# Moving the attention outputs and score maxima off TensorE's transposes and onto DMA, and dealing the freed places out again

## The reference

```
x = layernorm(x + self_attention(x))          # iterated three times, 16 heads of 16
x = layernorm(x + cross_attention(x, ctx))    # 1601 context rows a batch, 16 heads of 16
x = layernorm(x + ffn(x))                     # 8 encoders, the best by its loss picks one adapter

# cross attention, for each of 8 batches and 16 heads:
scores = (q @ k.T) / sqrt(16)                 # 512 x 1601
attn   = softmax(scores)                      # needs the maximum and the sum of each of 512 rows
out    = attn @ v                             # 512 x 16
x2     = (out of all heads, 512 x 256) @ Wo.T
```

## Time and profile before

| what | value |
|---|---|
| median of 3 runs | 1702.16 us |
| the profiled execution | 1697.87 us |
| its span, first to last instruction | 1696.1 us |
| mean granted TensorE clock | 0.991 |
| TensorE busy | 1619.5 us, 95% |
| VectorE busy | 1235.1 us, 73% |
| ScalarE busy | 1062.5 us, 63% |
| DMA engines, mean | 116.58 MB moved, 69 GB/s |

### The profile page before, as it was taken

The page is one execution under the profiler, slowest core; times in us unless marked ns, Lnnn a source line. Parts: engine busy times, 40 slices in busy tenths (PEclk is TensorE's granted clock), DMA queues, the critical chain, the costliest instruction groups (busy, mean ns, idle before and its releaser), DMA issues.

```text
span 1696.1 us, 25766 instructions
## 1 busy us (share of the span) xinstructions
PE 1619.5 (95%) x9848; PEld 607.4 (36%) x9848; DVE 1235.1 (73%) x1790; ACT 1062.5 (63%) x2012; POOL 161.5 (10%) x151
## 2 busy tenths in 40 slices
PE   6779999999999999999999999999999999999987
PEld 5442323432333334333334334333334333332234
DVE  6787777877778777877778767877778777776423
ACT  2227676766666666676666766676666766666651
POOL 7311000100010000100010000100001000000000
PEclk9889999999999999999999999999999999999999
DMA  5673170706135160715317070623407050420000
GB/s 154 118 161 71 34 137 5 127 25 121 43 68 91 54 105 12 128 37 104 60 42 109 21 134 24 102 63 81 82 9 131 25 86 26 83 31 2 4 25 16
DMA packets 101342, 116.58 MB, mean 69 GB/s; under 512 B 21834, under 2 KB 86987, under 8 KB 101220
## 3 DMA queue, kind: packets, MB, share of 16 engines
q1 hardware_dynamic: 98484, 113.89, 34.1%
q10 hardware_dynamic: 2736, 1.06, 0.3%
HBM read 80.12 MB, written 34.78 MB: 68 GB/s over the span
## 4 chain that ended last, share of the span: by engine, by line
PE 83%; DVE 6%; ACT 5%; issue 5%; DMA 1%; POOL 1%; ACTq 0%; SPq 0%; POOLq 0%; DVEq 0%
PE banks L1107 22%; PE values L1126 22%; PE banks L1081 11%; PE work L990 5%; PE work L1004 5%; ACT xprobs L1263 4%; PE work L947 4%; PE work L1011 3%; PE work L1017 3%; PE work L932 3%; DVE xneg_max_pieces L1451 2%; PE work L1020 1%; PE work L996 1%; PE work L1029 1%; DVE xv_rows L1409 1%
## 5 line engine op out<-in xcount | busy, mean ns | idle before, releaser
L1263 ACT ACTIVATE xprobs<-banks 128x512 f32<-128x512 f32 x1664 | 902.4, 595 | 440.5 <-PE banks L1107 425.6
L1451 DVE TENSOR_REDUCE xneg_max_pieces<-banks 128x2 f32<-128x1024 f32 x768 | 910.0, 1220 | 273.2 <-PE banks L1081 271.1
L1107 PE MATMUL banks<-xq_stacks,xk_stacks 99*128 99x512 bf16 (+1 forms) x1664 | 523.3, 385 | 16.2 <-ACT xprobs L1263 8.5
L1126 PE MATMUL values<-xprobs,xv_rows 128*17 128x512 f32 x3328 | 437.9, 598 | 1.0 <-ACT xprobs L1263 1.0
L1107 PEld LDWEIGHTS banks<-xq_stacks,xk_stacks 99*128 99x128 bf16 (+1 forms) x1664 | 128.9, 97 | 412.3 <-ACT xprobs L1263 281.3
L1081 PE MATMUL banks<-xk_stacks,xq_stacks 49*128 49x512 bf16 (+1 forms) x2048 | 249.7, 335 | 10.7 <-DVE xneg_max_pieces L1451 9.0
L1081 PEld LDWEIGHTS banks<-xk_stacks,xq_stacks 49*128 49x128 bf16 x2048 | 56.8, 94 | 273.7 <-DVE xneg_max_pieces L1451 156.0
L1518 POOL TENSOR_TENSOR xk_parts<-xk_rest,xk_parts 128x401 bf16<-128x401 f32 (+1 forms) x64 | 59.0, 921 | 705.4 <-ACT xk_parts L1224 705.4
L1126 PEld LDWEIGHTS values<-xprobs,xv_rows 128*17 128x17 f32 x3328 | 55.1, 95 | 120.4 <-issue 118.9
L1513 POOL TENSOR_TENSOR xrstd<-xrstd,mhalf 128x4 f32<-128x4 f32 x23 | 23.2, 1010 | 647.5 <-DVE xrstd L1323 647.5
L1004 PE MATMUL work<-xvT,ctxT_a 128*128 128x128 f32 (+1 forms) x416 | 57.2, 282 | 3.1 <-DVE xk_rest L1384 2.0
(11 more groups left out here) (301 smaller groups left out, 1062.6 us busy)
## 6 DMA issues: line engine op xcount, KB each, us to landing
xk_stacks<-key_parts_dram SPq DMA_DIRECT2D x186, 200.1 KB, 11.8
key_parts_dram<-xk_parts SPq DMA_DIRECT2D x144, 100.0 KB, 1.7
xq_stacks<-parts_dram SPq DMA_DIRECT2D x186, 64.0 KB, 8.1
ctxT_a<-in_ctxT SPq DMA_DIRECT2D x4, 1601.0 KB, 7.2
ctxT_b<-in_ctxT SPq DMA_DIRECT2D x4, 1601.0 KB, 7.5
parts_dram<-xq_parts SPq DMA_DIRECT2D x45, 128.0 KB, 2.0
key_parts_dram<-xk_parts SPq DMA_DIRECT2D x48, 100.2 KB, 4.8
xa<-in_x SPq DMA_DIRECT2D x8, 512.0 KB, 14.2
```

The costliest lines, as they stand in the source:

```text
L1107: pe.matmul(scores[n % SRING], kst[0:ROWS[par], k, h2, par, t * P:(t + 1) * P], qst[0:ROWS[par], k, h2, par, :], start=True, stop=True).th ...
L1126: last = pe.matmul(av[32 * j:32 * j + HD + 1, :], vals[:, k, t, gr * GH + j, :], probs[:, sl % 2, j, :], start=t == 0, stop=t == XKT - 1)
L1263: nc.scalar.activation(probs[:, sl % 2, j, :], scores[n % SRING], ACT.Exp).then_inc(exped, 1)
L1451: nc.vector.tensor_reduce(nmp[:, of % 2, j2, :, q, piece], pairs[n % MRING][:, :, :], AX.X, ALU.max, negate=True).then_inc(on["mxr"], 1)
```

## The change: what it does

- The jobs `otr`, `oT` and `max` are gone. IN_BETWEEN keeps one job (`v` 3, now in slot 19).
- `x1T`, `x2T` (two each) and `loss` are moved from IN_BETWEEN to slot ends of their own. To make the room, `xo` 0, `xo` 1, `qproj` 0 and `mid` go from 2 parts to 1, and `gram` 2 from 3 to 2. SLOT_END is put in a new order.
- The outputs of a group go from `oS` by four DMAs of 16 rows into `oT` (dims by tokens), with the sums spread by a fifth over 128 partitions. VectorE inverts 16 columns (`invert`), SyncE sends the inverses to DRAM and reads them back, each row 16 times, and VectorE multiplies (`scale`, 64 partitions x 512). `xo` reads `oT`.
- The maxima are turned by VectorE (a transpose in blocks of 32 x 32, one more step of `dve_max_parts`), and SyncE, not ScalarE, sends them to DRAM and into the stack (`sp_max_rows`).
- In the last group all four scores stand ahead of the products and go through a ring of 6 banks.
- At the end of the program only the last group's outputs are still turned on TensorE; the half of `xo` that doesn't need them is done before.

```
-        IN_BETWEEN = {
-            1: ("otr", 3, PREV), 2: ("oT", 0, PREV), 4: ("oT", 1, PREV), 8: ("x1T", 0, NEXT), 10: ("max", 1, NOW),
-            11: ("x1T", 1, NEXT), 12: ("x2T", 0, PREV), 14: ("otr", 0, NOW), 16: ("x2T", 1, PREV), 18: ("v", 3, NOW),
-            23: ("max", 2, NOW), 27: ("otr", 1, NOW), 35: ("loss", 0, PREV), 36: ("max", 3, NOW),
-            41: ("otr", 2, NOW), 49: ("max", 0, NEXT),
-        }
+        IN_BETWEEN = {19: ("v", 3, NOW)}
         SLOT_END = [
+            (("kproj", 0, NEXT), 1), (("kproj", 1, NEXT), 1), (("v", 0, NOW), 2), (("v", 1, NOW), 2),
+            (("xo", 0, PREV), 1), (("xo", 1, PREV), 1), (("x1T", 0, NEXT), 1), (("x1T", 1, NEXT), 1),
...
         VECTOR_WORK = {
+            1: [("invert", "o", 3, PREV)], 4: [("aggr", "x1", 0, NEXT)],
+            14: [("invert", "o", 0, NOW)], 18: [("scale", "o", 0, NOW)],
+            27: [("invert", "o", 1, NOW)], 32: [("scale", "o", 1, NOW)],
+            40: [("invert", "o", 2, NOW)], 44: [("scale", "o", 2, NOW)],
+            5: [*norm_steps("apply", "x1", 0, 2, NEXT), ("scale", "o", 3, PREV)],
...
+            elif name == "invert":
+                m = GROUPS * b + q
+                v.wait_ge(moved, N_MOVED * (m + 1))
+                v.reciprocal(rs[:, m % 2, :], rs[:, m % 2, :]).then_inc(inverted, 1)
+            elif name == "scale":
+                v.wait_ge(spread, 16 * (m + 1))
+                v.tensor_tensor(oT[these, k, :], oT[these, k, :], rsb[these, :], ALU.mult).then_inc(scaled, 1)
...
+        def sp_max_rows(of):
+            sp.wait_ge(on["comb_ready"], n)
+            sp.dma_start(g.max_dram.rearrange("r (b c) -> b r c", c=32), mrow[:]).then_inc(on["mrow_out"], 16)
+            sp.wait_ge(on["mrow_out"], 16 * n)
+            for par in range(2):
+                sp.dma_start(qst[row:row + 2, k, gr * GH // 2:(gr + 1) * GH // 2, par, :], src[par])
...
+        def sp_move_outputs(m):
+            sp.wait_ge(evac, m + 1)
+            sp.dma_start(rs[:, m % 2, :], oS[HD::2 * HD, :].rearrange("j (s x) -> j s x", x=GH * T // P)).then_inc(moved, 16)
+            for j in range(GH):
+                row = half * P // 2 + j * HD
+                sp.dma_start(oT[row:row + HD, k, :], oS[2 * HD * j:2 * HD * j + HD, :]).then_inc(moved, 16)
+
+        def sp_spread_inverses(m):
+            sp.wait_ge(inverted, m + 1)
+            sp.dma_start(g.rsum_dram[m % 2].rearrange("j (s x) -> (j s) x", x=GH * T // P), rs[:, m % 2, :]).then_inc(rs_out, 16)
+            sp.wait_ge(rs_out, 16 * (m + 1))
+            sp.dma_start(rsb[these, :], g.rsum_dram[m % 2].unsqueeze(1).broadcast_to([GH, HD, T])).then_inc(spread, 16)
...
+        def score_bank(n):
+            if n < LAST_SCORE:
+                return scores[n % SRING], SRING
+            place = n - LAST_SCORE
+            return g.banks[:, place % LAST_RING, :], before
...
             elif name == "xo":
                 if part == 0:
-                    pe.wait_ge(on["w_free"], ph.order.after(("oT", 1, b)))
-                last = rows_of(W, x2T, xoT, i, units(part, parts, 2 * CH))
+                    pe.wait_ge(scaled, GROUPS * (b + 1))
+                last = rows_of(W, oT, xoT, i, units(part, parts, 2 * CH))
```

More of the change, by code:

```diff
@@ L1158, in act_job @@
             name, i, b = job
-            on_scalar = ("oT", "x1T", "x2T", "kproj", "qproj", "enc", "mid", "wdT", "gw", "x1T head", "qproj rest",
+            on_scalar = ("x1T", "x2T", "kproj", "qproj", "enc", "mid", "wdT", "gw", "x1T head", "qproj rest",
                          "qproj head")
@@ L1369, in dve_job @@
             name, i, b = job
-            on_vector = ("kproj", "qproj", "xo", "y", "gram", "loss", "max", "otr", "qproj rest", "qproj head")
+            on_vector = ("kproj", "qproj", "xo", "y", "gram", "loss", "qproj rest", "qproj head")
             if name not in on_vector and not (name == "v" and not ph.first):
@@ L1491, in dve_slot @@
             if parts:
[L1492 to L1493 removed]
+                for step in range(1, 4):
+                    dve_max_parts(MAIN, m + 1, step)
             if todo:
@@ L1617, in sp_stacks @@
                 sp_query_stacks(c, top)
+                if top and between is not None:
+                    sp_spread_inverses(between)
                 sp_key_stacks(b, c, top)
@@ L2001, in dve_front @@
                 if n == MXG:
-                    for step in range(3):
+                    for step in range(4):
                         dve_max_parts(FIRST, 0, step)
-                    dve_job(FIRST, ("max", 0, 0))
                 elif n - 1 in BETWEEN_TILES and n < MXG:
@@ L2041, in cross_attention_and_ffn @@
         tail_w = (g.W[:], g.banks[:, 4, :])
+        tail_oT = (g.banks[:, 4, :], g.banks[:, 5, :])
+        tail_xo = [g.banks[:, q, 0:D] for q in range(QT)]
+        ox = rsb.rearrange("p (q n) -> p q n", q=QT)
         tail_enc = [g.banks[:, i, :] for i in range(NPAIR)]
@@ L2050, in pe_tail, with xo @@
             pe.wait_ge(loop["w_free"], len(MAIN.order.names))
+            def xo(c, first, last):
+                for q in range(first, last):
+                    one = pe.matmul(tail_xo[q], oT[:, c, q * P:(q + 1) * P], xoT[:, c, :], start=c == 0, stop=c == CH - 1)
+                return one
+            pe.wait_ge(scaled, B * GROUPS - 1)
+            xo(0, 0, 2)
             pe.wait_ge(evac, B * GROUPS)
             transposes(g.W[:], oS[:].rearrange("p (q n) -> p q n", q=QT), 0).then_inc(t_otr_made, 1)
+            xo(0, 2, QT)
             pe.wait_ge(t_ox_in, 1)
-            for c in range(CH):
-                transposes(tail_w[c], ox, c).then_inc(t_oT_made, 1)
-            for one in t_oT_in:
+            for q in range(QT):
+                one = pe.transpose(tail_oT[q // 2][:, q % 2 * P:(q % 2 + 1) * P], ox[:, q, :], ident[:])
+                if q % 2:
+                    one.then_inc(t_oT_made, 1)
+            for i, one in enumerate(t_oT_in):
                 pe.wait_ge(one, 1)
-            for i in range(2):
-                rows_of(tail_w[i], x2T, xoT, i, range(2 * CH)).then_inc(t_xo_made, 1)
+                xo(1, 2 * i, 2 * i + 2).then_inc(t_xo_made, 1)
             pe_keep_busy(pe, KEEP_NORM, g.banks[:, 5, :])
```

207 lines of the change are left out of this document (111 added, 96 removed).

## The result

| kernel | median | lowest to highest | against before, 95% interval |
|---|---|---|---|
| before | 1701.23 us | 1699.74 to 1702.57 | |
| changed | 1655.38 us | 1651.15 to 1656.91 | 0.9727, 0.9706 to 0.9748 |

A forecast was written before the change was run, and what follows sets the result against it. TensorE bounds the kernel, slot by slot. Full batches -27, batch 0 -5, batch 7 -4.4, last group -5.4, end -2.0, start -1.3 sum to -45 us: 1655 us forecast, own range 1647 to 1664, 8-in-10 range 1641 to 1674.

The forecast's parts named there:

- The slot rule: Loop slots: 0.99 + what stands in between + 0.54 + the larger of 1.88 and TensorE's own work, in us.
- 1.88 is no floor: Rival: slots with a short job at the end take 3.2 in place of 3.41 us; 1640 us, chance 0.07.
- Transposes, `loss`, merges: Full batch: ten transpose sets leave in between at 0.60 each, -6.0; `loss` -0.8; five merged jobs at 0.80, +4.0 us.
- Waits that go: Full batch: waits vanish in slot 12 (0.66), slot 51 (0.53) and at `max` in slots 10 and 49; together -2.0 us.
- New waits: Full batch: `scale` delays `xo` 0 in slot 6, +0.3; VectorE's transpose of the maxima, slots 47 to 51, +0.4; together +0.7 us.
- DMA cover: Moves before `invert`: a landing of 2.9 us is free, 0.8 more absorbed by the pairs' ring; landing taken as 2, cost nothing.
- The slower rival: `invert` in slots 1, 14, 27, 40 waits for the moves; landing above 3.7 us paid 31 times, 1726 at 6; chance 0.05.
- a sign of being wrong: Idle time before `invert` that ends with a DMA would show the prediction wrong.
- The last group: 13 slots fall from 40.0 to 34.6 us, -5.4, with six banks and 2.23 us for four exponentials in a jobless slot.
- Batch 7: Up to slot 38: seven transpose sets, three `max`, `loss` and a slot 12 wait go, three merges cost; -4.4 us.
- Start and batch 0: Batch 0 gains 5 us; the start gains 1.3 as ScalarE stops issuing the first maxima's DMAs (bounds +2 and -3).
- A second sign named for being wrong: A group's first score waiting for the maxima would show the prediction wrong.

The follow-up runs named there:

- experiment 7: Changed kernel with `x1T`, `x2T`, `loss` back in between, `xo` 0, `xo` 1, `qproj` 0, `mid` in two parts and `gram` 2 in three: median 1654.62 us.
- Experiment 5: Changed kernel with ScalarE's queue again issuing the maxima's DMAs for 31 of 32 groups: median 1666.75 us, ratio 0.9796 to the kernel before.
- experiment 4: Changed kernel with all four `invert` of a batch one slot earlier (slots 0, 13, 26, 39): one run, 1689.40 us.
- experiment 3: Changed kernel with `invert` waiting only for the sums' DMA, on a semaphore of its own, not for all five moves: one run, 1656.96 us.
- experiment 6: Changed kernel with the last group issued like all others, through the ring of two banks instead of six: one run, 1659.27 us.
- Experiment 10: The changed kernel itself, unedited, run again beside the fastest follow-up version on the same chip: median 1657.62 us, ratio 0.9748 to the kernel before.

## Why the prediction was right, point by point

The six full batches, -27.2 against -27, were right by their parts. That the total came within 0.4 us of the forecast is luck: the misses below have both signs, and the changed kernel's second median is 1657.62.

- *The slot rule* held. `x1T` slots take 3.41, `xo` 1's slot 4.23, slots 12 and 51 have no wait. The rival "1.88 is no floor" fell in slot 9.
- *Transposes, `loss`, merges.* The sizes 0.60, 0.8 and 0.80 are those that experiment 7 measured backwards (0.59 to 0.66, 0.77, and 0.81 but for `mid`, 0.66). No run puts `otr` and `oT` back; that they cost the same is read from the slots they left, slot 27 from 4.00 to 3.41 and slot 2 from 3.90 to 3.32.
- *Waits that go*, -2.0. Slot 12 fell to 4.22, slot 51 by 0.51, and slots 10 and 49 each by 0.49 with `max` itself. Experiment 5 shows that 1.5 us a batch would hang on ScalarE's issues in the changed kernel; 0.5 of it, in slot 38, wasn't there before. The Trainium skill, page "DMA: Bandwidth & Descriptors", section "Issuing engines are not separate DMA queues", calls the time saved by issuing elsewhere usually small beside the DMA. Here it is not small, 1.25 us beside a landing of 1.4, and giving it back cost 8.9 us behind batch 0: the measurement decides against it.
- *New waits*, +0.7 in sum and measured 0.76, but with the places mis-sized. The one of slot 6 was put at 0.3 and is 0.57. The cluster of slots 47 to 51, put at 0.4, costs nothing: the maxima's transpose on VectorE takes 0.21 us. Instead slot 13 takes 3.60: ScalarE has the copy of the values and that of the queries' second bf16 part in a row ahead of two exponentials there, and TensorE waits 0.22 us for the first of them. That wait wasn't foreseen.
- *DMA cover.* The five moves took 3.1 us of issues in three groups of four and landed 1.39 us after the last, close to the nearest row, 1.4, where I had taken 2. The slower rival stayed small, with less room than I wrote: I had SyncE free once the values are copied out, and for group 2 it isn't. Once a batch VectorE does wait for a DMA, 0.8 to 1.4 us, which I had named as a sign of being wrong, and it costs nothing; experiment 4 shows that one slot earlier most of the gain is lost. From the Trainium skill, the same page, section on why a DMA increments its semaphore by 16 (4 engines) and specifications (pieces under 512 bytes), I had worked out that the sums would be the last to land; experiment 3 shows them landed 1.31 us after their own issue in one batch, and before the last move.
- *The last group*, -5.4 and measured -6.8. The failed term is 2.23 us for four exponentials. It was read from a first start to a last end. The timeline of the changed kernel has three in a row:

```profile
1589.52 1.57 ACT L1258 ACTIVATE xprobs<-banks 128x512 f32<-128x512 f32 x3
```

  (1.57 - 0.60) / 2 = 0.49 from start to start, so 1.96 a slot, and 1.96 is what the eight slots take. `mid` (3.82) and `y` (3.35) were put 0.2 too low each.
- *Batch 7*, -4.4 and measured -3.1. The wait of `x2T` 0 for VectorE's normalisation is gone, as counted. But slot 13 takes 4.17 in place of 3.41, for TensorE's pairs wait there for VectorE, which has the normalisations between its maxima:

```profile
1479.91 0.39 PE L1080 MATMUL banks<-xk_stacks,xq_stacks 49*128 49x512 bf16 x2 [0.58 <-DVE xneg_max_pieces L1437]
```

  The other 0.44 is slot 38, which takes 3.31 in place of 2.87 because of the last group's ring (experiment 6).
- *Start and batch 0*, -6.3 and measured -4.2 in the first profile and -1.2 in the second. Slot 1 of batch 0, 1.2 and 0.9 longer than before, is one part of the miss, slots 38 and 39 are another. Experiment 10 shows that one profile can't tell: the stretch varies by 6 us. The term of -1.3 for the start can be neither confirmed nor denied. A second sign named for being wrong did show: in batch 0 a group's first score waits for the maxima, 0.3 us in one profile and 3.7 in the other.

## What to carry to other kernels

In a loop where one engine sets the pace, find what its slot costs bare, in between and at the end, and price each move by place, not by its own length: the same four transposes cost 0.6 us in one place and nothing in another. A path that leaves the bounding engine for DMA is free as long as the waiting instruction stands far enough behind the landing; look at the margin at each place, since the cost comes abruptly (here 1.0 to 1.8 us of waiting were free and 4.1 cost 3.0), and look at the granted clock behind a long wait, since two of the waits of some 4 us cost 4.6 and 5.7. Then read the slots that are longer than the rule says: taking out the waits of slots 6 and 11 and dealing five jobs back brought a full batch from 189.6 to 188.2 and the median down by another 0.8%, of which some 9 us of 13 lie behind batch 0.

## What the runs showed of the hardware

- A write of 8 KB by SyncE's queue had landed 1.4 us after its issue in 21 of the changed kernel's 32 groups, and 3.1 to 8.4 us after it in some places where the stacks of half a batch had been issued ahead of it.
- The issue of a DMA with 16 rows takes SyncE 0.57 to 0.63 us, in some cases up to 1.6, so five in a row cost more (3.1 us and up) than the landing of the last (1.39).
- An exponential of 128 x 512 shows a duration of 0.60 us, and follows the one before after 0.49.
- TensorE's granted clock fell to 0.50 in the loop in five of the twelve profiles, each time right behind a wait that had left TensorE idle (experiments 4 and 10); it cost 1.6 us in slot 39 of batch 0 and 4.3 us over two batches of experiment 4. Waits of like length left it at 1.00 in other batches.
- Nearly all of the spread between executions seen here is in the start and batch 0; 1355.36 and 1355.40 us behind them in two runs.
